# The residual addition of the second attention, moved from GpSimd to VectorE

## The chip, the cores and the metric

The kernel runs on 1 core of one Trainium2 chip. The metric is the device time of one execution in microseconds (us); the time of a kernel is the median over its runs. The text speaks of TensorE (PE), VectorE (DVE), ScalarE (ACT), GpSimd (POOL) and SyncE (SP), which run beside each other and wait for each other through semaphores.

## What is computed

A post-norm decoder layer over 16 sequences of 256 tokens with 256 features, all in float32. The first half is a linear attention and a cross attention over a context. The second half, which this case is about, works along the batch axis: a normalisation, an attention of 16 heads (4 heads of keys and values) over the 16 tokens that stand at one position, a residual addition, a second normalisation, and a mixture of 8 experts of which each token takes 2:

```python
ln1_out = _layernorm(hidden_states, ln1_weight, ln1_bias)
# q, k, v from ln1_out; causal softmax attention over the axis of 16
hidden_after_attn = hidden_states + proj_out
ln2_out = _layernorm(hidden_after_attn, ln2_weight, ln2_bias)
# logits, softmax, top 2 of 8 experts; gelu(x @ w1) @ w2 for each, weighted
return hidden_after_attn + moe_out
```

The caller normalises `x + that` once more. So the input `x` is wanted at the very end as well as its attention result: what the last stage adds to the experts' results is `x + hidden_after_attn`.

## The kernel before, in words

The program has four stages: keys of the context, the two attentions of the first half, the attention along the batch axis (`batch_axis_attention`, 254 to 441 us in the trace), and the experts (`experts`, from there to the end).

In the third stage the 4096 tokens are 8 groups of 4 tiles of 128 tokens (GROUPS = 8, NI = 4). `resid` holds all rows of `x` in SBUF (128 partitions, 32 tiles of 256 numbers and one more). The stage is a pipeline written out by hand: each engine has its own list of steps, and in iteration n it works on several groups at once. Nothing reorders them: each engine runs its own list from the top, and a step that waits holds up all behind it on that engine.

VectorE in iteration n: softmax of group n (L1241 to L1254), keys and values of group n+1 (L1216, L1229), the statistics of the second normalisation for group n-1 (L155, L158), the choice of experts for group n-2 (`route_pick`, L1275 to L1298, whose last results are `hot` and `picked`), the addition `h_rows = attention + resid` for group n (`add`, L1266, two instructions of 128x512), and the rows' places for group n-2 (`route_slots`, L1303 to L1318, whose last result is `slot_u`).

GpSimd in iteration n: the first three tiles' scatters of group n-3 (`send_rows`, L949, an indirect DMA whose descriptors GpSimd makes; two for each tile, so six), then `root` for group n-1 (L1038 to L1042, four instructions on 128x4, one a power of -0.5), then `residual` for group n-1 (L1052, two instructions of 128x512 that add `h_rows` into `resid`), then the two scatters of the fourth tile of group n-3. Scatters begin with n = 3.

What hangs on these steps: ScalarE waits for `root` before it makes the normalised rows (`second_rows`, L1094). TensorE turns these rows (L1361, "turning h" below), then counts places from `picked` (L1468, L1470), and then computes the next group's scores (L1392, L1399), for which the next iteration of VectorE waits with its first instruction, L1241. The product that `add` waits for is L1449 (`attended`, x32). `add` for group n also waits (`keep_done`) until `resid` and `h_rows` are through with `residual` of group n-1, since it overwrites `h_rows`. In the last iteration, n = 7, the order on TensorE is another: there the count of places for group 5 stands ahead of `attended`.

After the last iteration, VectorE does the statistics of group 7, `route_pick` and `route_slots` of group 6, splits two blocks of the experts' weights (L901), and routes group 7. GpSimd does six scatters of group 5, `root` of group 7, the last two of group 5, sixteen of groups 6 and 7, and `residual` of group 7. The experts' stage waits for all sixteen signals `keep_done` at its start on ScalarE, and at the end on VectorE.

## Time and profile before

| what | value |
|---|---|
| median of 3 runs | 788.13 us (785.64 to 791.9) |
| the profiled execution | 791.32 us, its span 789.6 us |
| busy share of the span | TensorE 80%, VectorE 68%, ScalarE 50%, GpSimd 41% |
| third stage, from its first to its last work on TensorE | 254 to 441 us |
| `residual` on GpSimd | 16 instructions, median 1180 ns |
| `add` on VectorE | 16 instructions, median 692 ns |

A row of a timeline gives start and duration in us, the engine, the line of the kernel, what is written from what, and, where the engine stood idle before, for how long and what released it. TensorE's granted clock is given as a share of its full 2.4 GHz. All durations come from the one profiled execution.

### The profile page before, as it was taken

To read this page: it belongs to the slowest core of one execution; us is meant where nothing else is said; L and a number is where in the kernel's file an instruction comes from. 1 tells how busy PE (TensorE), PEld (TensorE's weight loads), DVE (VectorE), ACT (ScalarE), POOL (GpSimd) and SP (SyncE) were. 2 spreads that over 40 slices of the span, in tenths; PEclk is the share of its full clock that TensorE was granted. 3 is DMA by queue.
4 is the path that set the end of the run, shared out by engine and by line. 5 is a ranking of instruction groups with operands and counts; after the bars stand their busy time and mean duration, and the time that the engine had idled before them with its cause. 6 is when DMAs were issued, how large, how long until landed. Compare 5 with 4: busy or idle time off the path is not lost.

```text
span 789.6 us, 19124 instructions
## 1 busy us (share of the span) xinstructions
PE 628.5 (80%) x5128; PEld 536.9 (68%) x5137; DVE 539.7 (68%) x1853; ACT 391.5 (50%) x923; POOL 321.0 (41%) x439
## 2 busy tenths in 40 slices
PE   4889999999961989999965139999999999997000
PEld 3678998898840667777755128888888888886000
DVE  1337878887855466888884836777777777775772
ACT  1335666656625556666534415555555555553233
POOL 0025777677643002566676722222222222222431
PEclk9989999999985899999976559999999999999555
DMA  6062444344311000111111422222222222221873
GB/s 196 0 177 71 143 133 113 106 138 123 97 28 27 1 2 2 42 56 57 56 56 68 154 91 70 72 80 68 79 68 79 69 80 68 80 68 47 279 245 114
DMA packets 48605, 69.19 MB, mean 88 GB/s; under 512 B 10577, under 2 KB 35281, under 8 KB 48561
## 3 DMA queue, kind: packets, MB, share of 16 engines
q1 hardware_dynamic: 40144, 46.30, 20.1%
q0 software_dynamic: 6480, 17.87, 6.1%
q10 hardware_dynamic: 1936, 4.46, 2.0%
q8 instruction: 24, 0.39, 0.2%
q14 instruction: 21, 0.16, 0.1%
HBM read 40.21 MB, written 24.19 MB: 82 GB/s over the span
## 4 chain that ended last, share of the span: by engine, by line
PE 42%; DVE 11%; DMA 5%; issue 3%; ACT 3%; POOL 3%; SPq 2%; DVEq 0%; POOLq 0%; ACTq 0%
PE half_bank L145 9%; PE half_bank L147 9%; PE half_bank L146 9%; PE half_bank L1856 5%; DMA out_dram<-all_w 3%; PE half_bank L1373 2%; PE half_bank L1837 2%; PE half_bank L1449 2%; POOL dispatched L949 2%; PE half_bank L1361 1%; DVE region_k_diag L1216 1%; ACT all_w L1615 1%; PE half_bank L1460 1%; DVE region_v_turned L1229 1%; DVE region_prob L1244 1%
## 5 line engine op out<-in xcount | busy, mean ns | idle before, releaser
L1675 POOL DMA_INDIRECT results<-all_w_qkv,ex_home x71 | 68.3, 961 | 200.6 <-DVE all_w_qkv L1800 170.5
L1707 ACT ACTIVATE region_hid_hi<-half_bank 128x256 fp32r<-128x256 f32 x142 | 46.9, 381 | 79.3 <-PE half_bank L1856 79.2
L949 POOL DMA_INDIRECT dispatched<-all_xh,all_slot_u x64 | 68.6, 1072 | 34.0 <-DVE all_slot_u L1318 17.4
L145 PE MATMUL half_bank<-region_w_hi,region_hid_hi 128*128 x284 | 81.2, 286 | 1.1 <-DVE region_hid_lo L1792 1.1
L146 PE MATMUL half_bank<-all_w,region_hid_hi 128*128 x284 | 79.7, 281 | 0.0
L147 PE MATMUL half_bank<-region_w_hi,region_hid_lo 128*128 x284 | 79.4, 280 | 0.0
L1694 ACT ACTIVATE all_xh<-half_bank,all_ln_b,all_ln_w 128x128 f32<-128x128 f32 x142 | 57.8, 467 | 21.0 <-PE half_bank L1837 21.0
L1800 DVE TENSOR_SCALAR all_w_qkv<-half_bank,ex_gate 128x256 f32<-128x256 f32 x71 | 34.3, 483 | 48.7 <-PE half_bank L147 48.7
L145 PE MATMUL half_bank<-region_w_hi,region_x_hi 128*128 x142 | 62.9, 443 | 0.7 <-DVE region_x_lo L1785 0.7
L1701 ACT ACTIVATE all_w_proj<-half_bank 128x512 f32<-128x512 f32 x71 | 42.5, 599 | 40.0 <-PE half_bank L147 40.0
L145 PEld LDWEIGHTS half_bank<-region_w_hi,region_hid_hi 128*128 128x128 f32 x284 | 53.3, 188 | 11.3 <-issue 7.8
L147 PE MATMUL half_bank<-region_w_hi,region_x_lo 128*128 x142 | 57.0, 402 | 0.0
L146 PE MATMUL half_bank<-all_w,region_x_hi 128*128 x142 | 56.8, 400 | 0.0
L1792 DVE TENSOR_TENSOR region_hid_lo<-half_bank,region_hid_hi 128x256 fp32r<-128x256 f32 x142 | 53.5, 419 | 1.5 <-ACT region_hid_hi L1707 0.3
L146 PEld LDWEIGHTS half_bank<-all_w,region_hid_hi 128*128 128x128 f32 x284 | 53.6, 189 | 0.5
L147 PEld LDWEIGHTS half_bank<-region_w_hi,region_hid_lo 128*128 128x128 f32 x284 | 53.6, 189 | 0.0
L1373 PE MATMUL half_bank<-region_xn_t,all_w_qkv 128*64 128x256 f32 x384 | 46.1, 399 | 1.0 <-ACT region_xn_t L1101 1.0
L1837 PE MATMUL half_bank<-all_identity,all_xh 128*128 128x128 f32 x142 | 27.9, 279 | 23.7 <-DMA all_xh<-dispatched 22.7
L1856 PE MATMUL half_bank<-all_identity,all_w_proj 128*128 128x128 f32 x284 | 45.4, 283 | 0.7 <-ACT all_w_proj L1701 0.7
L1373 PEld LDWEIGHTS half_bank<-region_xn_t,all_w_qkv 128*64 128x64 f32 x384 | 28.6, 144 | 15.7 <-issue 2.1
L1615 ACT ACTIVATE all_w<-all_w,region_en_small 128x256 f32<-128x256 f32 x32 | 16.8, 590 | 44.0 <-DVE region_en_small L1593 24.0
L1856 PEld LDWEIGHTS half_bank<-all_identity,all_w_proj 128*128 128x128 f32 x284 | 30.6, 142 | 7.5 <-issue 4.9
(241 smaller groups left out, 1809.3 us busy)
## 6 DMA issues: line engine op xcount, KB each, us to landing
all_xh<-dispatched SPq DMA_DIRECT2D x71, 130.5 KB, 2.1
all_w<-in_moe_w_dram SPq DMA_DIRECT2D x32, 256.0 KB, 3.1
all_w<-results SPq DMA_DIRECT2D x12, 512.0 KB, 6.7
all_resid<-at_x SPq DMA_DIRECT2D x32, 128.5 KB
shared_x_t<-in_x_t_dram SPq DMA_DIRECT2D x16, 256.0 KB, 4.2
at_x_tok<-in_x_dram SPq DMA_DIRECT2D x16, 256.0 KB, 4.3
out_dram<-all_w ACTq DMA_DIRECT2D x6, 512.0 KB
dispatched<-all_tail SPq DMA_DIRECT2D x8, 261.0 KB, 3.3
```

The costliest lines, as they stand in the source:

```text
L145: nc.tensor.matmul(out, a_hi, b_hi, start=(start and i == 0), stop=False)
L146: nc.tensor.matmul(out, a_hi, b_lo, start=False, stop=False)
L147: ins = nc.tensor.matmul(out, a_lo, b_hi, start=False, stop=(stop and i == len(pairs) - 1))
L949: nc.gpsimd.indirect_dma_start(out=dram["dispatched"], out_offset=bass.IndirectOffsetOnAxis(ap=keep["slot_u"][g % SENDS][:, u, k:k + 1], a ...
L1373: ins = nc.tensor.matmul(out[HALF * i:HALF * (i + 1), :], w_qkv[:, c, which * HALF:(which + 1) * HALF], tiles[:, :, i, :], start=(c == 0), ...
L1675: nc.gpsimd.indirect_dma_start(out=dram["results"], out_offset=bass.IndirectOffsetOnAxis(ap=home[par][:, 0:1], axis=0), in_=ym[par], in_of ...
L1694: ins = nc.scalar.activation(xm_t[par][:, c, :], p_x[:, c, :], ACT.Identity, bias=keep["ln2_b"][:, c:c + 1], scale=keep["ln2_w"][:, c:c + 1])
L1701: nc.scalar.activation(hid[par], p_h[par][:, :], ACT.Gelu_apprx_tanh).then_inc(s["hid_ready"], 1)
L1707: nc.scalar.activation(hid_hi[par][:, cs, :], p_t[half], ACT.Copy).then_inc(s["hid_high"], 1)
L1792: V.tensor_tensor(hid_lo[par][:, cs, :], p_t[half], hid_hi[par][:, cs, :].bitcast(F32), ALU.subtract).then_inc(s["hid_split"], 1)
L1837: ins = nc.tensor.transpose(p_x[:, c, :], xm[par][:, c * P:(c + 1) * P], const["identity"][:, :])
L1856: ins = nc.tensor.transpose(p_t[half][:, c, :], hid[par][:, cols], const["identity"][:, :])
```

## The change

`residual` becomes a step of VectorE. In iteration n it stands directly behind the statistics of group n-1; for the last group it stands behind `route_slots` of group 6. GpSimd's list loses it. The lines of the changed kernel are 8 lower from there on, so that L1052 becomes L1267, L1266 becomes L1258 and L1275 becomes L1273.

```diff
@@ gpsimd_program
-        def residual(g):
-            pool.wait_ge(s["h_ready"], 2 * g + 2)
-            for i in range(2):
-                rows = resid[:, g * NI + 2 * i:g * NI + 2 * i + 2, 0:D]
-                nc.gpsimd.tensor_tensor(rows, rows, h_rows[:, 2 * i:2 * i + 2, :], ALU.add).then_inc(s["keep_done"], 1)
-
         for n in range(1, GROUPS):
             if there(n - 3):
                 scatter(n - 3, range(0, 3))
             root(n - 1)
-            residual(n - 1)
             if there(n - 3):
                 scatter(n - 3, range(3, NI))
...
         scatter(GROUPS - 1, range(NI))
-        residual(GROUPS - 1)
@@ vector_program
+        def residual(g):
+            dve.wait_ge(s["h_ready"], 2 * g + 2)
+            for i in range(2):
+                rows = resid[:, g * NI + 2 * i:g * NI + 2 * i + 2, 0:D]
+                nc.vector.tensor_tensor(rows, rows, h_rows[:, 2 * i:2 * i + 2, :], ALU.add).then_inc(s["keep_done"], 1)
+
...
             if there(n - 1):
                 second_statistics(n - 1)
+                residual(n - 1)
             if there(n - 2):
                 route_pick(n - 2)
...
         route_pick(GROUPS - 2)
         route_slots(GROUPS - 2)
+        residual(GROUPS - 1)
         weights.make_low(dve, "w1", E - 1)
```

On VectorE this is the place between values and routing in an iteration from n = 2 on; before the change it reads (L158 is the end of the statistics, L1275 the start of `route_pick`):

```order
L1229 TENSOR_TENSOR region_v_turned<-half_bank,all_own_kv 128x8x64 x2
L155 BN_STATS ba_stats_h<-region_h_rows 128x6 x4
L158 BN_AGGR ba_mv_h<-ba_stats_h 128x2 x4
L1275 COPY ba_logits<-half_bank 128x32
L1278 MAX ba_best<-ba_logits 128x8 x4
```

and with the change:

```order
L1221 TENSOR_TENSOR region_v_turned<-half_bank,all_own_kv 128x8x64 x2
L155 BN_STATS ba_stats_h<-region_h_rows 128x6 x4
L158 BN_AGGR ba_mv_h<-ba_stats_h 128x2 x4
L1267 TENSOR_TENSOR all_resid<-all_resid,region_h_rows 128x2x256 x2
L1273 COPY ba_logits<-half_bank 128x32
```

The whole of `route_pick`, and `add` behind it, now stand behind two more instructions of 128x512.

On GpSimd this is an iteration of the loop's middle, before:

```order
L1038 TENSOR_SCALAR ba_var<-ba_mv_h 128x4
L1040 TENSOR_TENSOR ba_rstd_h<-ba_var,all_minus_half 128x4
L1041 TENSOR_TENSOR ba_mean<-ba_mv_h,ba_rstd_h 128x4
L1042 TENSOR_SCALAR ba_shift_h<-ba_mean 128x4
L1052 TENSOR_TENSOR all_resid<-all_resid,region_h_rows 128x2x256 x2
L949 DMA dispatched<-all_xh,all_slot_u 34816x261 x8
```

and with the change:

```order
L1038 TENSOR_SCALAR ba_var<-ba_mv_h 128x4
L1040 TENSOR_TENSOR ba_rstd_h<-ba_var,all_minus_half 128x4
L1041 TENSOR_TENSOR ba_mean<-ba_mv_h,ba_rstd_h 128x4
L1042 TENSOR_SCALAR ba_shift_h<-ba_mean 128x4
L949 DMA dispatched<-all_xh,all_slot_u 34816x261 x8
```

The eight scatters (two of one group and, behind a wait, six of the next) now follow `root` directly.

## Rows read from the trace of the kernel before

**Rows 1.** Windows, iteration 5: length, busy us (count) PE, PEld, DVE, ACT, POOL; clock
```profile
364.00:383.40 19.40, 17.75 (x264) 14.28 (x263) 17.00 (x54) 12.21 (x25) 12.56 (x14) 1.00 0.17 58
```

**Rows 2.** Timeline of VectorE, iteration 5: start, duration, engine, line, operation
```profile
374.89 0.38 DVE L158 BATCH_NORM_AGGREGATE ba_mv_h<-ba_stats_h 128x2 f32<-128x6 f32 x4
...
377.30 1.38 DVE L1295 TENSOR_TENSOR ba_hot<-all_xh,all_experts 128x32 f32<-128x32 f32 x2
378.71 1.02 DVE L1298 TENSOR_TENSOR ba_picked<-ba_hot 128x32 bf16<-128x32 f32 x1
379.77 0.69 DVE L1266 TENSOR_TENSOR region_h_rows<-half_bank,all_resid 128x512 f32<-128x512 f32 x1
...
383.37 0.68 DVE L1241 TENSOR_REDUCE ba_top<-half_bank 128x32 f32<-128x512 f32 x1
```

**Rows 3.** Timeline of GpSimd, iteration 5: root and residual
```profile
375.44 0.23 POOL L1038 TENSOR_SCALAR ba_var<-ba_mv_h 128x4 f32<-128x4 f32 x1 [2.67 <-DVE ba_mv_h L158]
375.75 1.04 POOL L1040 TENSOR_TENSOR ba_rstd_h<-ba_var,all_minus_half 128x4 f32<-128x4 f32 x1
...
377.37 2.31 POOL L1052 TENSOR_TENSOR all_resid<-all_resid,region_h_rows 128x512 f32<-128x512 f32 x2
```

**Rows 4.** Timeline of VectorE, iteration 7: the same two lines
```profile
413.53 0.29 DVE L1295 TENSOR_TENSOR ba_hot<-all_xh,all_experts 128x32 f32<-128x32 f32 x2
413.86 0.19 DVE L1298 TENSOR_TENSOR ba_picked<-ba_hot 128x32 bf16<-128x32 f32 x1
```

**Rows 5.** Timeline of VectorE: softmax's last product, 128x512, two inputs in SBUF
```profile
389.50 0.69 DVE L1254 TENSOR_TENSOR region_prob<-region_prob,ba_rec 128x512 f32<-128x512 f32 x1
```

**Rows 6.** Timeline of GpSimd: a scatter made beside it
```profile
389.62 1.40 POOL L949 DMA_INDIRECT dispatched<-all_xh,all_slot_u  x1 [0.30 <-issue]
```

**Rows 7.** Timeline of TensorE: the products for `add`, iterations 2, 5, 6 and 7
```profile
316.53 3.73 PE L1449 MATMUL half_bank<-all_w_proj,region_o_t 64*128 64x256 f32 x32 [0.20 <-issue]
...
375.76 3.72 PE L1449 MATMUL half_bank<-all_w_proj,region_o_t 64*128 64x256 f32 x32 [0.20 <-issue]
...
394.13 3.72 PE L1449 MATMUL half_bank<-all_w_proj,region_o_t 64*128 64x256 f32 x32 [0.20 <-issue]
...
414.15 0.26 PE L1470 MATMUL half_bank<-ba_picked,all_ones 128*128 128x32 bf16 x4
414.92 6.16 PE L1449 MATMUL half_bank<-all_w_proj,region_o_t 64*128 64x256 f32 x32 [0.51 <-issue]
```

**Rows 8.** Timeline of VectorE: first instruction of `add`, iterations 2, 4 and 6
```profile
320.54 0.69 DVE L1266 TENSOR_TENSOR region_h_rows<-half_bank,all_resid 128x512 f32<-128x512 f32 x1
...
360.26 0.69 DVE L1266 TENSOR_TENSOR region_h_rows<-half_bank,all_resid 128x512 f32<-128x512 f32 x1 [0.47 <-PE half_bank L1449]
...
399.29 0.69 DVE L1266 TENSOR_TENSOR region_h_rows<-half_bank,all_resid 128x512 f32<-128x512 f32 x1
```

**Rows 9.** Timeline of TensorE: turning h in iterations 1 and 5, scores in 5
```profile
301.94 1.09 PE L1361 MATMUL half_bank<-all_identity,all_xh 128*128 128x128 f32 x8
...
379.65 1.09 PE L1361 MATMUL half_bank<-all_identity,all_xh 128*128 128x128 f32 x8 [0.16 <-ACT all_xh L1094]
...
381.23 1.16 PE L1399 MATMUL half_bank<-region_k_diag,region_q_t 64*64 64x64 f32 x64
```

**Rows 10.** Timeline of ScalarE, iteration 1: the normalised rows
```profile
299.82 2.08 ACT L1094 ACTIVATE all_xh<-region_h_rows,ba_shift_h,ba_rstd_h 128x256 f32<-128x256 f32 x4 [0.74 <-POOL ba_shift_h L1042]
```

**Rows 11.** Timeline of VectorE: start of iteration 2, and routing of group 7
```profile
304.61 0.69 DVE L1241 TENSOR_REDUCE ba_top<-half_bank 128x32 f32<-128x512 f32 x1 [0.72 <-PE half_bank L1399]
...
437.68 0.19 DVE L1275 COPY ba_logits<-half_bank 128x32 f32<-128x32 f32 x1 [1.48 <-PE half_bank L1460]
```

**Rows 12.** Chain of waits around the last groups: start, duration, what
```profile
413.92 2.30 POOL all_resid L1052 x2
...
424.11 0.96 POOL dispatched L949
...
426.40 0.24 POOL ba_var L1038
```

## Prediction

> **What bounds the kernel now.** I read the windows first, then the timelines of VectorE, GpSimd and TensorE in one iteration of the third stage, then the chain of waits to its end. In iteration 5 of 19.4 us VectorE is busy for 17.00 and TensorE for 17.75 at full clock, GpSimd for 12.56 [rows 1]. The timeline of VectorE has nearly no gap there: the stage's inner iterations are bound by VectorE's list, with TensorE a fraction of a microsecond behind. GpSimd has room. At first sight a step that moves from GpSimd to VectorE should cost its full length. Two things speak for a closer look.
>
> First, VectorE's routing. L1295 (two instructions of 128x32) takes 1.38 us and L1298 (one) 1.02 us in iteration 5 [rows 2]; in iteration 7 the same lines take 0.29 and 0.19 [rows 4]. In iteration 5 GpSimd's residual runs from 377.37 to 379.68 [rows 3], over both; L1298 ends at 379.73, as it ends. In iteration 7 the residual only starts at 413.92 [rows 12], behind L1295. So the residual on GpSimd holds up VectorE's small additions by (1.38 - 0.29) + (1.02 - 0.19) = 1.92 us an iteration, in iterations 2 to 6, which have both steps.
>
> Second, the end. From iteration 7 on the chain of waits leaves VectorE and goes through GpSimd: the residual of group 6, 2.30 us from 413.92, then scatters of 0.96 us each without a pause, and only then the root of group 7 at 426.40 [rows 12], for which ScalarE, TensorE and the last routing wait.
>
> **The change part by part.** *VectorE gets two instructions of 128x512 with both inputs in SBUF.* The nearest row is L1254, of the same size and kind: 0.69 us, and the next instruction (at 390.11 in that timeline) starts 0.61 us later [rows 5]. Two cost 1.22 to 1.38; I take 1.26. *VectorE loses the hold-up*, 1.92. From the statistics to the end of routing the list gets 1.92 - 1.26 = 0.66 us shorter.
>
> *What of this arrives.* `add` needs L1449 as well. In iteration 2 L1449 ends at 316.53 + 3.73 = 320.26 and add starts at 320.54; with 0.06 for the wait 0.22 can be gained. In iteration 5 the end is 379.48, add starts at 379.77: 0.23. In iteration 6 it is 397.85 against 399.29: all 0.66 [rows 2, 7, 8]. In iteration 4 add already waits for L1449, 0.47 us [rows 8]: nothing. Iteration 3 I count as nothing too. So at most 0.22 + 0.23 + 0.66 = 1.1 us.
>
> *What it takes on the other side.* VectorE's residual starts at the end of the statistics (374.9 + 0.38 = 375.27), just as `root` starts on GpSimd (375.44) [rows 2, 3]. Do the two disturb each other? It can be seen for a scatter: beside L1254, which ends at 390.19 [rows 5], a scatter started at 389.62 takes 1.40 in place of 0.96 [rows 6, 12]: 0.44 more, 0.13 short of the 0.57 for which L1254 still ran. Other scatters that meet a VectorE instruction with two inputs in SBUF have the same pattern. By this, L1038 at 375.44 waits for the first of the new instructions (ends at about 375.9): 0.3 us; and L1040, then due at about 376.1, for the second (ends at about 376.5): 0.3 more. Root is late by 0.66, with a lower bound of 0 (a 4-element instruction might slip between) and an upper one of 1.3 (both instructions entire). In the other direction I take nothing: while L1040 runs, 375.75 to 376.79 [rows 3], VectorE's list goes on without a stretched instruction.
>
> The Trainium skill says more (SBUF — State Buffer, "Who interferes with whom"): a VectorE instruction with two SBUF inputs and a GpSimd instruction that reads SBUF exclude each other for the whole length of whichever came first. The trace agrees for the residual on GpSimd. The same section infers that making descriptors is not held up by such an addition; the stretched scatters of this trace say otherwise. By the strict rule root would be late by up to 1.3 us, the second rival below.
>
> *Who waits for root.* ScalarE's rows and then TensorE's turning. In iteration 1 ScalarE ends at 299.82 + 2.08 = 301.90 and TensorE starts turning at 301.94 [rows 9, 10]; scores follow, and VectorE waits 0.72 us for them [rows 11]. There is no slack: iteration 1 gets longer by root's whole lateness, 0.66. (VectorE's own residual costs nothing there; it has no routing and waits for L1449 anyway.) In iteration 5 turning starts at 379.65, after 0.16 of waiting for ScalarE, and scores end at 381.23 + 1.16 = 382.39, while VectorE takes them at 383.37 [rows 2, 9]: 0.98 of slack. With root late by 0.66 scores end at 383.05, and VectorE would come at 383.14: the 0.23 survives. In iteration 6, of the same lengths, VectorE gains 0.66 but the scores lose 0.66 of the 0.98, so 0.98 - 0.66 - 0.07 for the wait = 0.25 is left. Sum up to iteration 7: +0.66 - 0.22 - 0.23 - 0.25 = -0.04.
>
> *Iteration 7 and the tail.* Here routing had no hold-up, so picked, which ends at 413.86 + 0.19 = 414.05, comes 1.26 later: 415.27 with the -0.04. The count of places stands ahead of L1449 on TensorE and takes about 0.36 with its wait (it ends at 414.41 now); L1449, now at 414.92 [rows 4, 7], starts at 415.63, 0.71 later. The statistics of group 7 follow it, now ready at 425.04 in the timeline; then at 425.75, and root of group 7 can start at 425.95. GpSimd meanwhile has lost 2.30 and its late root 6 gives back 0.66 less the 0.2 for which it was waiting for scatters; the places of group 5 come at about 416.9, so GpSimd is free at about 424.7. So root of group 7 starts at 425.95 in place of 426.40: -0.45, of which the 1.26 on VectorE has eaten most of the 1.6 that GpSimd's queue gave. The last residual, 1.26 plus L901, fits into VectorE's time before routing of group 7, which has 1.48 idle [rows 11], with 0.2 to spare; were that cover gone it would cost its 1.26 in full, since the tile table hangs behind. GpSimd's residual of group 7 stood behind all scatters and nobody on the chain waited for it. The experts' stage issues the same instructions as before; I carry the -0.45 to the end.
>
> **Sum**: +0.66 - 0.70 - 0.41 = about -0.45 us. The profiled execution takes 791.32 and would take 790.9; it lies 3.2 us above the median of the runs, 788.13, which becomes 787.7.
>
> **The rivals.** *The hold-up only changes sides at no price (0.17):* root isn't delayed. Then iteration 1 costs nothing and iterations 2, 5 and 6 bring 1.1: with -0.41 from the tail -1.5, 786.6. For it: L1038 is tiny. Against: [rows 5, 6]. *Root waits for both instructions entire (0.13):* late by 1.3. Iteration 1 loses 1.3; in 2, 3, 5 and 6 scores overtake VectorE's 0.98 of slack by 1.3 + 0.07 - 0.98 = 0.4 each; 4 has more slack. +2.9 - 0.41 = +2.5, 790.6. It decides once root is late by more than about 0.9. *Slower, the hold-up was not the residual's (0.05):* if L1295 and L1298 stay at 1.38 and 1.02 for another reason (root or scatters beside them), VectorE pays 1.26 in 2, 3, 5 and 6, and 1.26 - 0.47 in 4: +5.8; with +0.66 in iteration 1 and about +0.8 from iteration 7 it is +7.3, 795.4. The point from which it decides is a refund under 1.26 of the 1.92. Against it stand [rows 2 to 4]: same shapes, same neighbours but the residual. *TensorE's clock (0.07):* L1449 takes 6.16 in iteration 7 in place of 3.72 [rows 7]. Should the shifted waits leave it at the high level, the statistics come 2.4 earlier and GpSimd's queue, free at 424.7, sets root 7: -1.25 more, 786.4; should an inner iteration fall to the lower level instead, its products for `add` cost 2.4 more, 790.1.
>
> **How the numbers follow.** The forecast has 0.58, the rivals 0.17, 0.13, 0.05 and 0.07. The likeliest is 787.7. The bounds of root's lateness give 786.6 to 790.6, the clock 786.4 to 790.1; the three runs before spread over 785.64 to 791.9, so a median of a few runs can be off by 2 us downward too. Range 785.0 to 791.0, outside which I leave the slow rival and some of the spread. About 1%, 7.9 us, is what a measurement of this kernel can tell from no change. Only the slow rival comes near it: faster 0.02, same 0.93, slower 0.05.
>
> **What would show it.** Right: L1295 and L1298 at about 0.29 and 0.19 in every iteration; the new addition at 0.69; L1038 or L1040 stretched or late by 0.6 together; iteration 1 longer by 0.7, iterations 2 to 6 shorter by 0 to 0.3; `add` waiting for L1449 in 2 to 5; root 7 about 0.4 earlier and released by VectorE's statistics, no longer by scatters. Wrong: VectorE's additions stretched by GpSimd's root or by scatters, which now stand where the residual stood; L1241 waiting for scores in 5 and 6 by more than 0.1, which would be the second rival; or the experts' stage changing its length.

## The result

The changed kernel is slower. Its median is 791.27 us against 788.53 us for the kernel before (20 runs of each on one chip). One run of the changed kernel, 997.73 us at a granted clock of 0.63, is left out of the ratio, which comes to 1.0047, with a 95% interval of 1.0030 to 1.0064 (the two medians alone give 1.0035). That is within 1%, as forecast, but on the other side of no change, and 791.27 lies outside my range of 785.0 to 791.0. The profiled execution's span went from 789.6 to 792.8 us, +3.2.

Where the 3.2 us are can be read from two starts: the first tile turned in the experts' stage (L1837) and the last result scattered (L1675). Timeline rows, first of the kernel before, then of the changed one:

```profile
463.70 0.66 PE L1837 MATMUL half_bank<-all_identity,all_xh 128*128 128x128 f32 x2 [22.67 <-DMA all_xh<-dispatched]
...
727.62 0.96 POOL L1675 DMA_INDIRECT results<-all_w_qkv,ex_home  x1 [2.22 <-DVE all_w_qkv L1800]
```

```profile
464.84 0.66 PE L1837 MATMUL half_bank<-all_identity,all_xh 128*128 128x128 f32 x2 [22.71 <-DMA all_xh<-dispatched]
...
731.05 0.95 POOL L1675 DMA_INDIRECT results<-all_w_qkv,ex_home  x1 [2.21 <-DVE all_w_qkv L1800]
```

Up to the first turned tile the changed kernel loses 464.84 - 463.70 = 1.14 us. From there to the last result it takes 266.21 in place of 263.92: 2.29 us more, in a stage that the diff doesn't touch. What follows is 0.2 shorter. Both parts need a cause.

**The third stage.** Starts of `add`, in us, by iteration:

| iteration | 0 | 1 | 2 | 3 | 4 | 5 | 6 | 7 |
|---|---|---|---|---|---|---|---|---|
| before | 284.41 | 302.17 | 320.54 | 340.31 | 360.26 | 379.77 | 399.29 | 421.11 |
| changed | 284.36 | 302.53 | 321.47 | 341.44 | 361.47 | 381.84 | 401.87 | 423.71 |
| later by | -0.05 | 0.36 | 0.93 | 1.13 | 1.21 | 2.07 | 2.58 | 2.60 |

So every iteration got longer, not only the first. Iteration 5 of the changed kernel, VectorE (the rows that answer to [rows 2, 3]):

```profile
376.45 0.38 DVE L158 BATCH_NORM_AGGREGATE ba_mv_h<-ba_stats_h 128x2 f32<-128x6 f32 x4
376.74 1.26 DVE L1267 TENSOR_TENSOR all_resid<-all_resid,region_h_rows 128x512 f32<-128x512 f32 x2
...
380.06 0.29 DVE L1293 TENSOR_TENSOR ba_hot<-all_xh,all_experts 128x32 f32<-128x32 f32 x2
380.39 0.19 DVE L1296 TENSOR_TENSOR ba_picked<-ba_hot 128x32 bf16<-128x32 f32 x1
381.84 0.69 DVE L1258 TENSOR_TENSOR region_h_rows<-half_bank,all_resid 128x512 f32<-128x512 f32 x1 [1.26 <-ACT all_xh L1086]
```

The first four rows are as forecast: the residual costs 1.26, the hold-up is gone (0.29 and 0.19 in place of 1.38 and 1.02). The last is what I had not seen: VectorE is done at 380.58 and then stands idle for 1.26 us, and what it waits for is ScalarE's L1086, the normalised rows. GpSimd and ScalarE in the same iteration:

```profile
377.00 0.50 POOL L1038 TENSOR_SCALAR ba_var<-ba_mv_h 128x4 f32<-128x4 f32 x1 [3.78 <-DVE ba_mv_h L158]
377.58 1.33 POOL L1040 TENSOR_TENSOR ba_rstd_h<-ba_var,all_minus_half 128x4 f32<-128x4 f32 x1
...
379.28 0.24 POOL L1042 TENSOR_SCALAR ba_shift_h<-ba_mean 128x4 f32<-128x4 f32 x1
```

```profile
379.05 0.24 ACT L1150 ACTIVATE ba_shifted<-ba_shifted 128x40 f32<-128x40 f32 x1 [0.85 <-DVEq L1284]
379.64 2.07 ACT L1086 ACTIVATE all_xh<-region_h_rows,ba_shift_h,ba_rstd_h 128x256 f32<-128x256 f32 x4 [0.35 <-POOL ba_shift_h L1042]
```

L1038 takes 0.50 where it took 0.23, and L1040 1.33 where it took 1.04 [rows 3]: root is held up by 0.27 + 0.29 = 0.56 us beside VectorE's residual, in every iteration from 1 to 6. The rows start 379.64 - 376.83 = 2.81 behind the end of the statistics; before it was 377.52 - 375.27 = 2.25, the same 0.56 less. They end at 381.71, and `add` starts 0.13 later. The list of waits, 285 to 440 us of VectorE (waited for: us in total, times, longest), has it first but one; the two waits above it are those of iterations 0 and 7, which the kernel before has too:

```profile
DVE region_h_rows L1258 <- PE half_bank L1449: 10.6, 2, 6.4
DVE region_h_rows L1258 <- ACT all_xh L1086: 9.9, 6, 3.8
```

The code says why. `add` has three waits, for its bank, for `keep_done`, and `wait(dve, s["xh2_ready"], g)`: it overwrites `h_rows`, so ScalarE must have read them too. My front part named only the second.

Of the 0.86 us that iteration 5 adds in the table, about 0.36 is a wait of 0.60 ahead of one L1233, elsewhere 0.24; I found no cause for it. The small steps at 3 and 4 are the kernel before's: `add` stood 6.97 and 7.14 behind the values there, in place of 6.7 in 1, 2, 5 and 6, with TensorE's granted clock at its lower level (1.2 GHz) at 331.2 to 334.6 and 351.6 to 355.1. The changed kernel's trace has no such stretch between 262 and 408 us, so the 1.13 and 1.21 there are smaller than what the change itself costs.

**The tail** gives part of it back. In iteration 7 the count of places comes later still, as forecast, and the product for `add` behind it:

```profile
417.89 0.21 PE L1468 MATMUL half_bank<-ba_picked,all_prefix 128*128 128x40 bf16 x1 [1.62 <-DVE ba_picked L1296]
...
418.12 5.55 PE L1449 MATMUL half_bank<-all_w_proj,region_o_t 64*128 64x256 f32 x32
```

L1449 starts 418.12 - 414.92 = 3.20 us later than before [rows 7], 0.62 more than the 2.58 that the iteration began late. That `add` is only 2.60 late is luck: the granted clock is at its lower level at 406.3 to 419.9 before and at 408.2 to 421.9 with the change, so less of L1449 falls into it, and it takes 5.55 in place of 6.16. The start of root of group 7 on GpSimd:

```profile
427.81 0.23 POOL L1038 TENSOR_SCALAR ba_var<-ba_mv_h 128x4 f32<-128x4 f32 x1 [0.17 <-DVE ba_mv_h L158]
```

Root of group 7 is now released by VectorE's statistics, as forecast, and no longer stands behind scatters: it starts 0.16 behind their end at 427.65, against 1.36 (426.40 - 425.04) before. GpSimd's last scatter ahead of it ended at 427.64, so the two came at the same time and the queue had no more to give. So the 2.60 of `add` become 1.41 at root and 1.14 at the first turned tile.

**The experts' stage.** It starts at TensorE's lower level in both traces; the windows from 470 to 480 us, before and changed (the last figures but two are the granted clock):

```profile
470.00:480.00 10.00, 9.66 (x55) 8.78 (x56) 7.53 (x29) 4.70 (x12) 0.98 (x1) 0.77 0.13 40
```

```profile
470.00:480.00 10.00, 9.31 (x45) 7.72 (x44) 8.11 (x28) 4.69 (x11) 0.95 (x1) 0.68 0.07 20
```

The kernel before is at full clock 10.8 us behind its first turned tile, the changed one 11.7 behind. From the first to the eleventh tile's turning the changed kernel takes 38.28 us in place of 37.61, 0.67 more; the next 55 tiles, at a granted clock of 1.00 in both, take 198.85 in place of 197.30, 1.55 more; what follows differs by less than 0.1. So up to 0.67 of the 2.29 may be the clock's. Of the stretch at full clock there is this to see: the changed kernel has one wait on VectorE that the kernel before doesn't have (list of waits, 500 to 700 us, VectorE and TensorE's weight loads):

```profile
PEld half_bank L145 <- issue: 7.3, 37, 0.3
DVE ex_token L1778 <- DVE ex_gate L1771: 4.7, 28, 0.2
```

Before, the first of them is 5.1 us in 25 times and the second isn't there. In the timeline of the changed kernel two tiles make a turn of VectorE's loop, and the copy of the token (L1778) of the second one comes late, by the same amount each time:

```profile
547.28 0.17 DVE L1778 COPY ex_token<-all_xh 128x5 f32<-128x5 f32 x1
...
550.89 0.17 DVE L1778 COPY ex_token<-all_xh 128x5 f32<-128x5 f32 x1 [0.17 <-DVE ex_gate L1771]
```

L1771 starts at 550.56, 0.33 ahead of it. In the kernel before the same two rows of a turn are

```profile
541.32 0.16 DVE L1771 TENSOR_TENSOR ex_gate<-ex_hit_gate 128x1 f32<-128x1 f32 x1
541.53 0.17 DVE L1778 COPY ex_token<-all_xh 128x5 f32<-128x5 f32 x1
```

that is 0.22 apart (median of 30 turns), so L1778 comes 0.11 late in each turn. Over the some 27 turns of the 55 tiles that is at most 3.0 us, of which 1.55 arrive. L1771, its neighbour, takes 0.16 in both; nothing of the data differs. What differs is where the loop stands: in the compiled program it has 47 instructions on VectorE, and 1048 stand ahead of it in place of 1032, since `residual` adds 16 to VectorE's list ahead of it.

### The profile page after: what moved, and what is told of

It reads as the page before. It is cut to its first block, busy times and chain, and to the rows that moved or that the text cites. A ratio compares the mean times of both kernels' runs of the same rounds, so it can differ in the third digit from the quotient of the medians.

```text
span 792.8 us, 19124 instructions
## 1 busy us (share of the span) xinstructions
PE 627.2 (79%) x5128; PEld 533.4 (67%) x5137; DVE 537.8 (68%) x1869; ACT 391.6 (49%) x923; POOL 303.4 (38%) x423
## 4 chain that ended last, share of the span: by engine, by line
PE 36%; DVE 13%; DMA 6%; POOL 4%; ACT 4%; issue 4%; DVEq 0%; SPq 0%; POOLq 0%; ACTq 0%
PE half_bank L145 9%; PE half_bank L147 9%; PE half_bank L146 8%; PE half_bank L1856 5%; DMA out_dram<-all_w 4%; POOL dispatched L949 2%; PE half_bank L1837 2%; ACT all_xh L1086 2%; DVE ba_stats_h L155 1%; DVE region_prob L1236 1%; DVE ba_top L1233 1%; DVE ba_total L1244 1%; DVE region_h_rows L1258 1%; PE half_bank L1449 1%; POOL ba_rstd_h L1040 1%
## 5 line engine op out<-in xcount | busy, mean ns | idle before, releaser
L1675 POOL DMA_INDIRECT results<-all_w_qkv,ex_home x71 | 68.0, 957 | 204.2 <-DVE all_w_qkv L1800 165.2
L145 PE MATMUL half_bank<-region_w_hi,region_hid_hi 128*128 x284 | 81.5, 287 | 1.0 <-DVE region_hid_lo L1792 1.0
L145 PE MATMUL half_bank<-region_w_hi,region_x_hi 128*128 x142 | 63.0, 443 | 0.5 <-DVE region_x_lo L1785 0.5
L145 PEld LDWEIGHTS half_bank<-region_w_hi,region_hid_hi 128*128 128x128 f32 x284 | 53.6, 189 | 13.3 <-issue 10.4
L1837 PE MATMUL half_bank<-all_identity,all_xh 128*128 128x128 f32 x142 | 27.9, 279 | 23.8 <-DMA all_xh<-dispatched 22.7
```

The lines of the kernel that those rows point to most:

```text
L145: nc.tensor.matmul(out, a_hi, b_hi, start=(start and i == 0), stop=False)
L1675: nc.gpsimd.indirect_dma_start(out=dram["results"], out_offset=bass.IndirectOffsetOnAxis(ap=home[par][:, 0:1], axis=0), in_=ym[par], in_of ...
L1837: ins = nc.tensor.transpose(p_x[:, c, :], xm[par][:, c * P:(c + 1) * P], const["identity"][:, :])
```

## Experiments

Two theories were to be tested. **A**: the third stage's loss is root, held up by VectorE's two-input additions, which arrives through ScalarE's rows at `add`. **B**: the experts' loss is the place of VectorE's loop in its program. Rivals: for A, that two instructions more in the list or the later gates (L1150 stands ahead of the rows on ScalarE and waits for VectorE) do it; for B, that the residual's move itself or the chip does it.

The runs were on other chips than the result's, and there also the kernel before is slower (medians 794.72, 798.33 and 796.47 in the three sessions). All 12 traces taken there have something that the result's two traces do not: from iteration 3 to iteration 6 ScalarE stands idle once or twice an iteration, mostly for 2.4 to 4.6 us in all, ahead of its copies of the queries and of the turned probabilities, and nothing in the profile releases it ("remote"). In `c_before`:

```profile
371.39 1.08 ACT L1137 ACTIVATE region_prob_t<-half_bank 128x512 f32<-128x512 f32 x2 [3.11 <-remote]
```

TensorE's granted clock is 1.00 in that iteration; what ScalarE waits for isn't known. Behind it TensorE's L1449, and with it `add`, comes late. So for A I compare iterations 1 and 2, which have neither this wait nor the lower clock in any trace, and for B the stretch from the first turned tile to the last result.

### Both kernels again

`c_after` is the changed kernel, `c_before` the kernel before, unedited.

> The changed kernel once more, to see what of its two differences comes back. Theory 1 (third stage): add of VectorE waits for ScalarE's normalised rows, which are late by root's hold-up (about 0.55 us); add of iteration 7 starts 2.5 us later than before (423.7 in place of 421.1), of which 1.1 are left at the first tile of the experts. Theory 2 (experts): the experts' loop of VectorE, the same instructions placed 16 instructions further on, has a gap of 0.17 us in front of the copy of the token in every turn, and the stage from the first turning to the last results is 266.2 us in place of 263.9. Both theories: 3.0 to 4.0 us slower than before. Rival to theory 2: the experts' stage varies from execution to execution whatever the program; then its length here is anywhere from 263.5 to 266.5 and the gap has nothing to do with it.

> The kernel before itself, once more, to be profiled on this chip: it is the comparison for the four kernels that ran here. Both theories: ratio 1.000 within its interval. The instruction-placement theory (VectorE's loop of the experts stands at other addresses in the changed kernel, and one instruction of a turn comes late) says 0 to 2 of the 28 copies of a token (L1775's kin) have the 0.17 us idle ahead of them, and first turned tile to last result about 263.9 us. If the chip and not the placement made the gap in the four runs, 27 or 28 copies have it here too and the stretch takes 265 us or more.

Measured: `c_after` 1.0045 (1.0023 to 1.0066), `c_before` 1.0010 (0.9971 to 1.0048). In `c_after` the gap ahead of L1778 is there 27 times between 500 and 700 us and the stretch takes 265.36; in `c_before` there is none and it takes 263.92. Root's two rows in iteration 1 are 0.50 and 1.33 against 0.23 and 1.05. Both signs go with the kernel, not with the chip.

### Theory A: the residual later in the list

`r_late`:

```diff
                 second_statistics(n - 1)
-                residual(n - 1)
             if there(n - 2):
                 route_pick(n - 2)
                 if n == GROUPS - 1:
                     route_slots(n - 2)
+            if there(n - 1):
+                residual(n - 1)
```

> The changed kernel with VectorE's residual moved from behind the statistics to behind the choice of experts, ahead of add. Theory 1: root on GpSimd meets no long addition and the gates' exponential is not late, so ScalarE's rows are as early as before; L1293 and L1296 at 0.29 and 0.19; add starts within 0.1 us of where it did before in each iteration, in iteration 6 too (held by ScalarE at 399.1), and in iteration 7 the picked experts are no later than before, so root of group 7 is about 1.1 us earlier than before (425.2 in place of 426.4). Third stage 1.1 to 1.5 us shorter than before, 2.2 to 2.6 shorter than with the change. The experts' loop lies as in the changed kernel: +2.3 by theory 2. Together +1 us against before (0.5 to 1.5). Rival (VectorE's list, not ScalarE's rows, sets the iteration; root's lateness is hidden): no better than the changed kernel in iterations 2 to 6.

Measured: 1.0016 (0.9989 to 1.0043). Iteration 2, VectorE, then GpSimd:

```profile
318.75 0.19 DVE L1296 TENSOR_TENSOR ba_picked<-ba_hot 128x32 bf16<-128x32 f32 x1
318.86 1.29 DVE L1267 TENSOR_TENSOR all_resid<-all_resid,region_h_rows 128x512 f32<-128x512 f32 x2
320.76 0.69 DVE L1258 TENSOR_TENSOR region_h_rows<-half_bank,all_resid 128x512 f32<-128x512 f32 x1 [0.62 <-ACT all_xh L1086]
```

```profile
316.55 0.23 POOL L1038 TENSOR_SCALAR ba_var<-ba_mv_h 128x4 f32<-128x4 f32 x1 [16.42 <-DVE ba_mv_h L158]
316.87 1.04 POOL L1040 TENSOR_TENSOR ba_rstd_h<-ba_var,all_minus_half 128x4 f32<-128x4 f32 x1
```

The residual now starts 0.34 after root is through (318.27 + 0.25), and root's rows are back at 0.23 and 1.04. `add` starts 6.58 behind the end of the values, against 7.14 in the changed kernel and 6.71 before: the whole loss of the iteration is gone, with the same two instructions still in VectorE's list. In iteration 1, where no routing stands between, root is held as in the changed kernel (0.50, 1.33) and `add` is at 7.08. That settles root against the length of the list. The gap of the experts' stage is there (27 times, 266.12 us), and here `add` still waits for ScalarE, so the saving stops at it. The third stage shorter by 1.1 us or more, which was expected too, can't be read from this trace: in iterations 3 to 6 ScalarE has the wait of unknown cause. The same goes for what was expected of `add` of iteration 7 in `f_one` and of the third stage in `n_none` below.

### Theory A: the same length with one SBUF input

`f_one` leaves out the residual; in its place stand two instructions of the same size that read `h_rows` alone:

```diff
-                rows = resid[:, g * NI + 2 * i:g * NI + 2 * i + 2, 0:D]
-                nc.vector.tensor_tensor(rows, rows, h_rows[:, 2 * i:2 * i + 2, :], ALU.add).then_inc(s["keep_done"], 1)
+                nc.vector.tensor_reduce(unused[:, i, :], h_rows[:, 2 * i:2 * i + 2, :], AX, ALU.add).then_inc(s["keep_done"], 1)
```

> Left out: the residual addition. In its place behind the statistics stand two reductions of the same 128x512 with one input in SBUF, of the same length (0.68 us each), with the same signals. It tells the hold-up of root apart from the mere place in the list. If the two inputs hold up GpSimd: root is 0.23 + 1.04 again in place of 0.50 + 1.33, 0.55 us earlier. If only the hold-up made the change dear, add starts as before. But the gates' exponential stands ahead of the rows on ScalarE and is 1.26 us later through the list in this run too; by that ScalarE's rows start 4.75 us behind the values on VectorE, against 4.45 before and 5.02 with the change, and half of the loss stays: add of iteration 7 about 1 us later than before. Rival (a reduction holds up GpSimd as well): root 0.50 + 1.33, as with the change.

Measured: 1.0021 (0.9993 to 1.0048). Iteration 2, VectorE, GpSimd and ScalarE:

```profile
314.60 1.25 DVE L1267 TENSOR_REDUCE ba_unused<-region_h_rows 128x2 f32<-128x512 f32 x2
...
319.22 0.69 DVE L1259 TENSOR_TENSOR region_h_rows<-half_bank,all_resid 128x512 f32<-128x512 f32 x1 [0.80 <-ACT all_xh L1087]
```

```profile
314.85 0.23 POOL L1039 TENSOR_SCALAR ba_var<-ba_mv_h 128x4 f32<-128x4 f32 x1 [16.43 <-DVE ba_mv_h L158]
315.17 1.04 POOL L1041 TENSOR_TENSOR ba_rstd_h<-ba_var,all_minus_half 128x4 f32<-128x4 f32 x1
```

```profile
316.89 0.24 ACT L1151 ACTIVATE ba_shifted<-ba_shifted 128x40 f32<-128x40 f32 x1 [0.83 <-DVEq L1284]
317.03 2.06 ACT L1087 ACTIVATE all_xh<-region_h_rows,ba_shift_h,ba_rstd_h 128x256 f32<-128x256 f32 x4
```

At the same place and length, root isn't held. What held it in the changed kernel is then the second input from SBUF, unless it is the output: the reductions also write only 128x2. No run separates the two for root, but scatters do. In the 14 traces 36 of them start while `add` runs, which has one input in SBUF and writes 128x512: they take 0.96 to 1.08, as undisturbed ones do. All 110 that start while the softmax's last product runs ([rows 5], two inputs in SBUF, the same output) take 1.23 to 1.41. The later gates are also to be seen, and their price: root is through at 316.82, the gates at 317.13, and the rows start 4.55 behind the values where `r_late` and the kernel before have 4.37 and 4.38 (4.75 was expected). So the gates would cost 0.17 an iteration, but only where root is early; in the changed kernel root is later than they are.

### Theory A: no residual at all

`n_none` leaves the residual out on every engine; VectorE raises `keep_done` in its place.

```diff
-                rows = resid[:, g * NI + 2 * i:g * NI + 2 * i + 2, 0:D]
-                nc.vector.tensor_tensor(rows, rows, h_rows[:, 2 * i:2 * i + 2, :], ALU.add).then_inc(s["keep_done"], 1)
+                dve.sem_inc(s["keep_done"], 1)
```

> The changed kernel with the residual addition left out altogether (its output lacks the second attention's residual); VectorE only raises the counter. Nothing on VectorE or GpSimd remains of it. By the theory that the hold-up of the diagonal root and the add's wait for ScalarE's rows make the third stage's loss: root at 0.23 and 1.04 us, iteration 1's add back at 302.0, rows behind the end of the values at 4.2 to 4.4 and the add at 6.4 to 6.7 in iterations 2 to 7, so the third stage is 0 to 1.5 us shorter than before's. VectorE's loop is placed as in the changed kernel or within a few instructions of it, so the gap of 0.17 us and its 2.3 us stay; ratio 0.999 to 1.003. The rival, that the third stage's rate is set elsewhere (TensorE's queue), has the adds as in before within 0.1 us each and ratio 1.003.

Measured: 1.0023 (0.9982 to 1.0064). Iteration 2, ScalarE, then VectorE:

```profile
315.46 2.07 ACT L1086 ACTIVATE all_xh<-region_h_rows,ba_shift_h,ba_rstd_h 128x256 f32<-128x256 f32 x4 [0.71 <-POOL ba_shift_h L1042]
```

```profile
315.76 0.19 DVE L1295 TENSOR_TENSOR ba_picked<-ba_hot 128x32 bf16<-128x32 f32 x1
317.67 0.69 DVE L1258 TENSOR_TENSOR region_h_rows<-half_bank,all_resid 128x512 f32<-128x512 f32 x1 [1.72 <-ACT all_xh L1086]
```

This is the run that shows what there was to gain. With neither the hold-up of 1.92 nor the residual's 1.26, VectorE waits 1.72 us for ScalarE, and `add` starts 6.61 behind the values: 0.10 earlier than before (6.71). In iteration 1 it is 6.53 against 6.67. The kernel before explains itself by its own rows in iteration 2, ScalarE, GpSimd and VectorE:

```profile
318.21 2.07 ACT L1094 ACTIVATE all_xh<-region_h_rows,ba_shift_h,ba_rstd_h 128x256 f32<-128x256 f32 x4 [0.69 <-POOL ba_shift_h L1042]
```

```profile
318.14 2.31 POOL L1052 TENSOR_TENSOR all_resid<-all_resid,region_h_rows 128x512 f32<-128x512 f32 x2
```

```profile
319.49 1.01 DVE L1298 TENSOR_TENSOR ba_picked<-ba_hot 128x32 bf16<-128x32 f32 x1
```

L1449 ends at 320.26 [rows 7], ScalarE's rows at 320.28, GpSimd's residual at 320.45, VectorE's list at 320.50, and `add` starts at 320.54 [rows 8]. Four things it needs end within 0.24 us. Taking away the last of them uncovers the next one.

### Theory B: only the place of the loop

`b_pad16` is the kernel before with 16 waits on VectorE, each long fulfilled, ahead of the experts' loop; `b_pad8`, `b_pad24` and `b_pad40` have 8, 24 and 40 of them.

```diff
+        for _ in range(16):
+            wait_apart(dve, keep["keep_done"], GROUPS * 2)
```

> The kernel before, with 16 waits on a semaphore that has long had its value, put on VectorE directly ahead of the experts' pipeline, where it stands idle for 9 us until the first rows come. The third stage is as before. Theory 2 (placement of the loop): the experts' loop then lies where it lies in the changed kernel, has the gap of 0.17 us in front of the token's copy, and the kernel is 2.3 us slower than before. Rival (the experts' stage is longer for what happened ahead of it, or by chance): no gap, 0 us, within 0.5.

Measured: 1.0047 (1.0021 to 1.0072), with the residual still on GpSimd and root and `add` of iteration 2 as before (0.23, 1.04; 6.71). VectorE's list of waits, 500 to 700 us:

```profile
DVE all_w_qkv L1800 <- PE half_bank L147: 34.1, 54, 0.8
DVE ex_token L1778 <- DVE ex_gate L1771: 4.7, 28, 0.2
DVE all_w_qkv L1800 <- issue: 0.6, 1, 0.6
```

and in its timeline:

```profile
546.40 0.17 DVE L1778 COPY ex_token<-all_xh 128x5 f32<-128x5 f32 x1 [0.17 <-DVE ex_gate L1771]
```

The stretch takes 265.21. So 16 instructions that do nothing make the gap in the kernel before, ahead of the same instruction. The medians differ by 3.2 us, of which the stretch shows only 1.3; where the rest is isn't shown (the interval starts at 1.7 us). `a_pad16` and `a_pad48` are the reverse, the same lines with 16 and 48 in the changed kernel, which puts the loop 32 and 64 behind its first place:

> The changed kernel with 16 more satisfied waits on VectorE ahead of the experts' loop, so that the loop stands 32 instructions later than before the change, where it stood 16 later. If the place of the loop's instructions decides, the 0.17 us gap ahead of the token's copy goes, or moves to another instruction of the turn; if it goes and none takes its place, the experts' stretch is back at about 264 us and the ratio to the kernel before is 1.0015 to 1.0025 (what the third stage lost alone, 1.2 to 2 us). If the residual's move itself (the list, the waits) makes the gap, it stays in 27 or 28 turns and the ratio stays at 1.0045.

> The changed kernel with 48 more satisfied waits, so that the loop stands 64 instructions later than before the change. If what matters is the place within a stretch of 64 instructions, this one stands as in the kernel before: no gap, the experts' stretch 263.9 us, ratio 1.0015 to 1.0025. If only instructions added ahead matter (the more, the worse), the gap is there and the ratio 1.0045 or more.

Measured: `a_pad16` 1.0007 (0.9973 to 1.0040), no gap, 263.71; `a_pad48` 0.9993 (0.9952 to 1.0033), no gap, 264.30. Root is held in both (0.51 and 1.32 in iteration 2) and `add` is late by as much as in the changed kernel (7.13, 7.14), so theory A's part is untouched. It doesn't show in their ratios, where 1.0015 to 1.0025 was expected. Adding instructions makes the changed kernel's last stage faster.

> The kernel before with 8 satisfied waits ahead of the experts' loop on VectorE. Placement by a boundary that one instruction of the loop crosses: at 8 the loop's instructions stand elsewhere than at 0 or 16, so the gap may sit ahead of another instruction of the turn or be absent; experts' stretch between 263.7 and 266. The rival, that a program that is longer by any amount up to 16 has it: the same 0.17 us ahead of the token's copy in 27 or 28 turns.

> The kernel before with 24 satisfied waits there. With 16 the gap was there, with the changed kernel's 16 plus 16 and plus 48 it was not: at 24 placement by a boundary says no gap ahead of the token's copy (it may be ahead of another instruction), and the stretch 263.7 to 264.5 us if none shows.

> The kernel before with 40 satisfied waits there. If the pattern repeats every 32 instructions, this one is like 8; if every 64, it is a position of its own. What is wanted is whether gap and length of the stretch go together once more: a gap of 0.17 us ahead of the token's copy with 265 us or more, or none with about 264.

Measured, one execution each: no gap ahead of L1778 in any of the three; 263.95, 264.12 and 264.20. VectorE's list of waits of `b_pad24`, the same stretch:

```profile
DVE all_w_qkv L1800 <- PE half_bank L147: 35.5, 55, 0.9
DVE all_w_qkv L1800 <- issue: 0.6, 1, 0.6
```

| loop later by (instructions) | kernels | gaps of 28 | stretch, us |
|---|---|---|---|
| 0 | before, `c_before` | 0 | 263.92, 263.92 |
| 8 | `b_pad8` | 0 | 263.95 |
| 16 | changed, `c_after`, `r_late`, `f_one`, `n_none`, `b_pad16` | 27 or 28 | 266.21, 265.36, 266.12, 265.01, 265.37, 265.21 |
| 24 | `b_pad24` | 0 | 264.12 |
| 32 | `a_pad16`, `rl_pad16` | 0 | 263.71, 263.86 |
| 40 | `b_pad40` | 0 | 264.20 |
| 64 | `a_pad48` | 0 | 264.30 |

(`n_none` raises a counter for each addition, so its loop stands where the changed kernel's does.) Gap and length go together in all 14 traces, and of the places tried only the one 16 later has them. The mean is 265.5 with the gap and 264.0 without: 1.5 us, between 1.0 and 2.3; the 2.3 of the first pair, which was expected of the later runs, was the largest. Ratios fall the same way: 1.0016 to 1.0047 with it, 0.9982 to 1.0010 without, though the single intervals overlap.

The 55 tiles at full clock separate the two groups better: 198.3 to 198.9 us with the gap, 197.2 to 197.6 without, 1.1 us in the mean, or a third of the 0.11 in each turn. The rest of the spread lies in the first ten tiles, which vary by half a microsecond and more in both groups (37.6 to 38.4 with it, 37.4 to 37.9 without).

The traces also say where the delay sits. Number VectorE's instructions from 0 as they stand in the compiled program, those of its sequencer included: the loop's 47 begin at 1032 in the kernel before. With 16 more ahead of it the late one, L1778, is the loop's 15th, number 1062. With 24 more (`b_pad24`) the copy isn't late, but a register operation of the sequencer (L75), the loop's 7th, is: it starts 0.24 us behind its neighbour in each of 30 turns, where all other kernels have 0.135. It is again number 1062, and the next instruction, which waits for a result anyway, hides it. With 8 more (`b_pad8`) number 1062 is the loop's 23rd, a copy (L1783), which is never less than 0.19 behind its neighbour, where the seven other kernels without the gap come down to 0.08 to 0.11. With none it is L1768, which waits for its neighbour's result for 0.18 in all kernels. With 32, 40 and 64 the whole loop lies behind 1062; nothing in it is late, and the first instruction behind its branch starts 0.19 behind the branch in place of 0.27. So what costs is one fixed place in VectorE's program inside the loop, and whether it costs anything depends on which instruction stands there.

### Both causes undone

`rl_pad16` is `r_late` with the 16 waits of `b_pad16`.

> Both causes undone at once: VectorE's residual behind the placing of the tokens (as in r_late) and 16 satisfied waits that move the experts' loop on by 16 instructions more (as in a_pad16). By the two causes (held root and late rows in the third stage; placement in the fourth) nothing of the loss is left but iteration 1's half microsecond: no gap ahead of the token's copy, 263.7 to 264.3 us of experts, rows 4.3 to 4.4 and add 6.6 us behind the values in iteration 2, ratio 0.999 to 1.001. If a third cause is at work (GpSimd's shorter program, VectorE's longer list by itself), the ratio is 1.002 or more with both undone.

Measured: 0.9982 (0.9950 to 1.0013). No gap, 263.86; iteration 2 has the rows at 4.37 and `add` at 6.58; iteration 1 is late as in the changed kernel (7.07). With both causes undone nothing measurable of the loss is left, and nothing measurable is gained over the kernel before: no third cause above 1 us, the upper end of the interval, and no version that can be said to beat it.

## Why the prediction was wrong

By its own steps:

- *VectorE's list, +1.26 and -1.92*: right in size. The additions took 1.26, the stretched lines are at 0.29 and 0.19 in every iteration.
- *Root late by 0.66*: right mechanism, size 0.56: 0.27 on L1038 and 0.29 on L1040, each a little less than the 0.33 assumed. `f_one` shows that it hangs on what the additions have and the reductions have not, and the scatters that this is the second SBUF input.
- *"What of this arrives"*: this is the first step that failed. It asked whether L1449 lets `add` start earlier, but `add` also waits for ScalarE's rows. The rows ended at 379.60 in iteration 5 before, 0.17 ahead of `add`, and at 399.11 in iteration 6, 0.18 ahead, where all 0.66 were counted as a gain; the row of L1094 in iteration 1 [rows 10] was read, but only for who waits on TensorE. `n_none` shows that at most 0.10 to 0.14 an iteration could arrive, not 0.22 to 0.66.
- *"There is no slack" in iteration 1, 0.98 of it later*: the slack of the scores was real (they held nobody up in iteration 5), but it was the wrong path. Root's lateness arrives by ScalarE's rows and `add` in iterations 2 to 6 as it does in 1: 0.41, 0.57, 0.50 and 0.51 in 1, 2, 5 and 6, where the kernel before has no lower clock (5 without its wait of unknown cause). The forecast had -0.04 up to the start of iteration 7; measured was +2.58.
- *Iteration 7*: `picked` later by 1.26 and L1449 by 0.71 was right in its mechanism (1.20 and 0.62 beyond the lateness of the iteration's start). It doesn't show in `add` only because TensorE's clock rose earlier within L1449, by luck.
- *The rival "root waits for both entire"* would have given +2.9 up to there, near the +2.6 found, but for another reason: root was late by 0.56, not 1.3, and the point "about 0.9" from which it was to decide came from the scores' slack.
- *The tail*: the release of root 7 by the statistics came as forecast. There the queue gave back 1.2 (2.60 became 1.41), as much as forecast (L1449 0.71 late, root 0.45 early). The last residual fitted in at no cost: the idle time ahead of L1273 fell from 1.48 [rows 11] to 0.27.
- *"The experts' stage issues the same instructions as before; I carry the -0.45 to the end"*: the second step that failed, and the larger one: +2.29 us in these traces. The same instructions at another place in the program took longer, by 1.1 us in the mean of 6 traces against 8 at full clock; 0.67 of the 2.29 lie in the first ten tiles, where the clock was still rising. It was named as a sign that would prove me wrong, but had no chance and no price.

Taken together: -0.45 forecast; +1.14 (first step, less the tail) and +2.29 (second step) found, less 0.2 behind them. That is 3.2 us of span; the medians differ by 2.7.

What stays open: what lies at number 1062 of VectorE's program; and why of 0.11 us in each turn about 0.04 arrive. TensorE's weight loads (L145) wait longer for "issue" with the gap (7.1 to 8.0 us in 36 to 43 times between 500 and 700 us, against 4.9 to 5.7 in 25 to 28 without), which says where the lateness arrives, not how. On the later chips the third stage's loss can't be seen in the total (`a_pad16` and `a_pad48` have it in iterations 1 and 2, at 1.0007 and 0.9993): behind ScalarE's wait of unknown cause `add` waits in iterations 3 to 7 for TensorE's L1449 (5 times in `c_after`, once in the result's trace), so that rows which are 0.56 late hold nobody up there. That this is why the total hides the loss is argued, not shown. So the third stage's share of the 0.47% is shown by the traces of the first chip alone.

## What to carry to other kernels

Before counting a shorter list as a gain, write down every wait of the instruction at its end and the time at which each was fulfilled; if several lie within a few tenths of a microsecond, removing one brings no more than its distance to the next (0.10 to 0.14 here), and one made later costs all but that. Put an elementwise instruction with two SBUF inputs on VectorE where GpSimd isn't about to start short work that others wait for: a few places down the list it was free. When a change adds or removes instructions ahead of a long loop, look at the loop for a small gap that recurs at one instruction, and try some padding before blaming the change itself.

## What the hardware showed that I had not expected

- Moving a loop in its engine's program is worth 0.1 to 0.3% of this kernel: an idle time of 0.17 us in place of 0.06 ahead of one of 47 instructions, at one of seven places tried, 1.0 to 2.3 us over 71 tiles. The delay of 0.11 stays at one number in the program (1062) and falls on whatever instruction the loop has there.
- The hold-up between VectorE and GpSimd also hits instructions on 128x4: 0.23 becomes 0.50 and 1.04 becomes 1.33 beside an addition of 128x512 with two SBUF inputs, and stays 0.23 and 1.04 beside a reduction of the same size with one. The Trainium skill (SBUF — State Buffer, "Who interferes with whom") has the two exclude each other for the whole instruction that came first. On GpSimd's side the traces agree but for 0.13 to 0.15 us: in iteration 5 L1038 starts with 0.41 of the first addition still to run and takes 0.27 longer, L1040 starts with 0.43 of the second to run and takes 0.29 longer, and the same holds for all 30 such powers.
- In the other direction a power of GpSimd on 128x4 holds up nobody. VectorE's L1280 has two inputs in SBUF and starts inside the 1.33 us of L1040 in the changed kernel's iteration 5:

```profile
378.69 0.19 DVE L1280 TENSOR_TENSOR ba_shifted<-ba_logits,ba_best 128x32 f32<-128x32 f32 x1
```

It takes 0.19, as in all 72 cases of the 14 traces. By that rule it would have waited until 378.91. GpSimd's own additions of 128x512 do hold VectorE's small ones to their end (1.38 and 1.02 in [rows 2]).
